# Local attention with its engine queues in another order: how six layers of a fused block on one NeuronCore respond

## The reference, cut to what matters

```python
qkv = x @ Wqkv                       # 128 -> 3 * 1024, 16 heads of 64
q = l2norm(q) * qs;  k = l2norm(k) * ksc
q = q * cos * scale + rotate_half(q) * sin * scale
k = k * cos / scale + rotate_half(k) * sin / scale
# windows of 32 tokens; each sees its own window and the one before
sim = einsum(q, k) * 8;  sim = where(mask, -big, sim)
out = einsum(softmax(sim), v)        # mask: it < jb or it > jb + 32
x = out @ Wo + x
```

## Time and profile before

| | |
|---|---|
| time of three runs | 8583.95, 8584.15, 8587.62 us; median 8584.15 |
| profiled execution | 8596.22 us, of which the span is 8594.4 us |
| period of one of the six layers | 530 to 531 us |
| one unit of attention in the steady part | 12.77 us |
| granted TensorE clock, whole span | 0.774 of full speed |

### The profile page before, as it was taken

The page is one execution under the profiler, slowest core; times in us unless marked ns, Lnnn a source line. Parts: engine busy times, 40 slices in busy tenths (PEclk is TensorE's granted clock), DMA queues, the critical chain, the costliest instruction groups (busy, mean ns, idle before and its releaser), DMA issues. The chain is left out here.

```text
span 8594.4 us, 84244 instructions
## 1 busy us (share of the span) xinstructions
PE 6067.9 (71%) x22816; PEld 3551.2 (41%) x22816; DVE 5534.0 (64%) x10124; ACT 3038.5 (35%) x6978; POOL 2830.0 (33%) x2050
## 2 busy tenths in 40 slices
PE   3686877868678686677766775677777775887554
PEld 1453544535455354122212221244555443665332
DVE  6775766757577575599848996477878776121334
ACT  1563655636456364100020001133333322333333
POOL 0452534525355252244413441044444442000000
PEclk6897989979899898699969997755555555555777
DMA  0000000000000000000000000000000000000000
GB/s 11 17 1 14 1 1 14 1 14 1 2 13 1 14 1 6 1 0 0 0 5 0 0 0 0 14 1 0 0 0 0 0 1 4 0 0 8 3 3 8
DMA packets 3953, 34.57 MB, mean 4 GB/s; under 512 B 401, under 2 KB 785, under 8 KB 2065
## 3 DMA queue, kind: packets, MB, share of 16 engines
q1 hardware_dynamic: 3600, 30.63, 1.0%
HBM read 29.58 MB, written 1.05 MB: 4 GB/s over the span
## 5 line engine op out<-in xcount | busy, mean ns | idle before, releaser
L744 POOL TENSOR_TENSOR slabs<-slabs 128x512 f32<-128x512 f32 x768 | 1034.7, 1377 | 1546.2 <-DVE slabs L680 1546.2
L1078 DVE TENSOR_TENSOR_SCAN slabs<-slabs 128x512 f32<-128x512 f32 x512 | 884.9, 1728 | 124.6 <-POOL slabs L1094 111.1
L1359 DVE MAX8 slabs<-slabs 128x8 f32<-128x512 f32 x1152 | 740.5, 687 | 295.1 <-ACT slabs L1310 285.3
L1094 POOL TENSOR_TENSOR slabs<-slabs 128x512 f32<-128x512 f32 x512 | 648.2, 1266 | 742.9 <-PE psum L1035 476.6
L1035 PE MATMUL psum<-slabs 128*128 128x512 f32 x1024 | 578.1, 646 | 296.5 <-POOL slabs L1094 296.5
L1393 POOL TENSOR_SCALAR slabs<-slabs 128x512 f32<-128x512 f32 x256 | 399.6, 1561 | 1043.0 <-DVE slabs L1366 1043.0
L629 ACT ACTIVATE slabs<-slabs 128x96 f32<-128x96 f32 x1536 | 553.0, 361 | 387.6 <-DVE slabs L709 387.6
L1275 PEld LDWEIGHTS psum<-slabs 128*128 128x128 f32 x3072 | 677.4, 333 | 7.5 <-ACT slabs L1301 7.5
L1275 PE MATMUL psum<-slabs 128*128 128x9 f32 (+1 forms) x3072 | 663.0, 359 | 0.0
L1261 PE MATMUL psum<-slabs 8*128 8x512 f32 (+1 forms) x768 | 596.9, 1136 | 79.7 <-DVE slabs L1342 58.5
L1269 PE MATMUL psum<-constants,slabs 128*128 128x128 f32 x1536 | 419.1, 433 | 274.3 <-POOL slabs L1397 263.7
(11 more groups left out here) (332 smaller groups left out, 11270.6 us busy)
## 6 DMA issues: line engine op xcount, KB each, us to landing
slabs<-F SPq DMA_DIRECT2D x6, 2756.5 KB, 10.2
weights<-S SPq DMA_DIRECT2D x4, 645.0 KB, 3.8
weights<-M SPq DMA_DIRECT2D x1, 2184.0 KB, 9.1
weights<-R SPq DMA_DIRECT2D x2, 1079.5 KB, 5.0
slabs<-x SPq DMA_DIRECT2D x1, 1024.0 KB, 4.8
slabs<-falloff SPq DMA_DIRECT2D x1, 1024.0 KB, 4.7
out<-slabs SPq DMA_DIRECT2D x1, 1024.0 KB, 3.9
weights<-L SPq DMA_DIRECT2D x1, 840.0 KB, 4.5
```

Of the source, the lines that this page charges most:

```text
L744: nc.gpsimd.tensor_tensor(out[:, at, :], normed[:, at, :], table, ALU.mult).then_inc(rope_done, 1)
L1078: nc.vector.tensor_tensor_scan(state[b % 2][:, 1:SEQ + 1], decay[:, cols(b)], fed[b % 2], 0.0, ALU.mult, ALU.add).then_inc(state_ready, 1)
L1094: nc.gpsimd.tensor_tensor(read[b % 2], r[:, cols(b)], state[b % 2][:, 0:SEQ], ALU.mult).then_inc(read_ready, 1)
L1359: nc.vector.max(eight, wk if k else s).then_inc(top_step, 1)
```

## The change

Four queues are reordered; no instruction is added or removed.

- PE: in iteration i `weigh` moves from the end of the iteration to the place between `turn_roped` and `score`, and works on unit i-3 instead of i-2. `values` moves from that place to the end.
- ACT: `square` comes first. `copy_values` works on unit i-1 and stands between `square` and `copy_turned`. `copy_context` moves from the head to behind `copy_turned`.
- DVE: `rope` for the keys of unit i and `total` for unit i-1 both stand at the end of iteration i. Written out, the sequence differs from that before in one thing: the reciprocal follows the key addition and no longer precedes it.

POOL's queue is the same.

```diff
# PE
-                if i < UNITS:
-                    values(i)
+                if i >= 3:
+                    weigh(i - 3)
                 if 1 <= i <= UNITS:
                     score(i - 1)
                 if 2 <= i <= UNITS + 1:
                     turn_probs(i - 2)
                 if i >= 3 and (i - 3) % 2 == 1:
                     project_out(i - 3)
-                if 2 <= i <= UNITS + 1:
-                    weigh(i - 2)
+                if i < UNITS:
+                    values(i)
# ACT
-                if i >= 3:
-                    copy_context(i - 3)
                 if i < UNITS:
                     square(i)
                 if 1 <= i <= UNITS:
+                    copy_values(i - 1)
                     copy_turned(i - 1)
-                if i < UNITS:
-                    copy_values(i)
+                if i >= 3:
+                    copy_context(i - 3)
                 if 2 <= i <= UNITS + 1:
                     copy_probs(i - 2)
# DVE
-                if 2 <= i <= UNITS + 1:
-                    total(i - 2)
-                if 1 <= i <= UNITS:
-                    rope(i - 1, 1, k_roped)
                 if i < UNITS:
                     normalise(i)
...
                 if i < UNITS:
                     rope(i, 0, q_roped)
+                    rope(i, 1, k_roped)
+                if 1 <= i <= UNITS:
+                    total(i - 1)
```

## The result

| | before | changed |
|---|---|---|
| median | 8587.62 us (5 runs, 8583.95 to 8590.67) | 8527.42 us (5 runs, 8515.90 to 8544.51) |
| ratio | | 0.9933, 95% interval 0.9918 to 0.9948 |
| profiled span | 8594.4 us | 8537.9 us |
| granted clock, whole span | 0.774 | 0.757 |

The change gains 60 us, 0.7%. The forecast was 154 us, and the measured time lies 27 us above the upper end of the range (8500).

The account below looks back on a forecast made before the run. A DVE and ACT loop of 12.78 us a unit was taken as the bound; per layer -26.1, -1.7 and +1.3 make -26.5, six layers -159, port +5: -154 us, forecast 8430 us, range 8395 to 8500.

Parts of the forecast that it names:

- The clock falls: Rival: new short pauses before weigh and key transposes halve PE's clock, +3.4 us a unit, kernel slower; chance 0.07.
- the 0.07: Chance given to the rival in which PE's clock falls and the kernel becomes slower.
- The clock was 1.00 through the steady part with pauses too: Argument against the falling-clock rival: PE in the kernel before had pauses, yet held full clock.
- PE's busy share rises: Argument against the falling-clock rival: PE's busy share goes from 0.81 to 0.88.
- Square first: ACT: square ahead of copy_context takes 1.21 us out of the loop, 12.78 to 11.57 us.
- Scores against the mask: PE to DVE: scores ready at 5.87 us after square's start, mask at 5.97; 0.1 us slack, lateness taken as 0.
- Project late in even iterations: PE: project, behind project_out and values, ends 0.5 us late in even iterations; pair 12.1 + 11.57 = 23.67 us.
- Copies moved back on ACT: ACT: copy_context done at 5.2 us and copy_probs at 7.75, both before the exponentials at about 8.7; no cost.
- The reciprocal behind the key addition: DVE and POOL: later finish_probs may delay small steps 0 to 0.35 us; 0.06 taken per odd unit, 5 us in all.
- keys gain some 0.1 us that nobody waits for: DVE: key addition ahead of the reciprocal gives turn_roped's keys some 0.1 us, with no effect on time.
- First and last units: Ends of each layer's attention: start -1.7 us (bounds 0 and -3.4), end +1.3 us (bounds -1.7 and +1.8).

Follow-up runs that it names:

- the fill: Changed kernel plus five unread products per unit on PE, two before the key-addition wait and three before weigh: 8394.62 us, ratio 0.9782.
- the five kernels of the table: Changed kernel without its DVE part 8573.5 us; as is 8527.4; with unread products before keys 8427.8, before weigh 8412.0, at both places 8394.6.

## Why the prediction was wrong, step by step

**The step that failed** is "The clock falls", as it was weighed and not as it was described. Its place was right (new short pauses, before weigh and before the key transposes), its price was close (3.4 us a unit forecast; 15.10 - 11.99 = 3.1 measured for a full dip, 13.62 - 11.99 = 1.6 for a partial one), and its threshold too: I put break-even at 8 of 28 units at half clock, and with 53 dips in six layers, 9 of 28, some of them partial, three quarters of the gain went. What was wrong is the 0.07, and both arguments for it. "The clock was 1.00 through the steady part with pauses too" compared single pauses: before there was one of 1.40 us ahead of the key transposes as well, but values stood right behind it. The trace of before shows it (L498 project, L509 the key transposes, L520 values; the scores follow at 385.10):

```profile
378.21 1.88 PE L498 MATMUL psum<-slabs 128*128 128x512 f32 x4
380.09 0.66 PE L506 MATMUL psum<-constants,slabs 128*128 128x128 f32 x4
382.15 0.66 PE L509 MATMUL psum<-constants,slabs 128*128 128x128 f32 x4 [1.40 <-DVE slabs L688]
382.65 1.88 PE L520 MATMUL psum<-slabs 128*96 128x512 f32 x4
```

The change put weigh there, which waits itself, and so three pauses came to stand with only eight transposes between them. "PE's busy share rises" compared averages over a unit, and rising it did (294.61 of 340 us, 0.87, some of it matmuls at half clock), while of the 3.45 us ahead of weigh 2.14 were idle. The rival was also bound to "and the kernel is slower": no case stood for a clock that falls in a third of the units and takes part of the gain, which is what came.

The Trainium skill, page "TensorE: Matmul & The Clock Gate", section "A second HAM failure mode: psum-queue depth-cycling", which the prediction set aside, says that short idles between groups of matmuls make the clock oscillate. The trace of the changed kernel agrees, with 0.50 and 1.00 in turn; the trace of before, with its pauses spread, held 1.00.

In numbers per layer: without dips the 28 intervals would take 14 x (11.54 + 11.99) = 329.4 us, 28.1 less than before, where I forecast 26.1. Measured they take 28 x 12.50 = 350.0. The dips cost 20.6 us a layer, 123 us in all. The spans of the profiled executions without and with the fill, 8537.9 and 8391.8 us, lie 146 us apart: 123 us are these intervals, and some 22 are the first three intervals of each layer, where the fill holds the clock too (in the first layer 1.00 between 270 and 300 us, against 0.79 in the changed kernel and 0.87 before).

**Square first:** right. The odd interval was forecast at 11.57 and is 11.54.

**Scores against the mask:** the tie held. With the first fill, in the steady part of the first layer, the mask never waits for the scores except once, at the layer's end.

**Project late in even iterations:** right, 0.45 us for the 0.5 forecast; the run with values behind project and the fill shows it, all intervals at 11.54.

**Copies moved back on ACT:** right as far as the time goes: the intervals of 11.54 us leave no room for a wait on them.

**The reciprocal behind the key addition:** right in the loop (1.47 us for finish_probs, L669's successor in the new file still 0.17 us, no effect alone), wrong in "keys gain some 0.1 us that nobody waits for". PE waited for them, 1.20 us with this part and 1.41 without, and with it the clock fell less often: 46 us.

**First and last units:** forecast -1.7 and +1.3 us a layer, measured about -0.4 for the first three intervals (38.0 for 38.4 us) and -0.6 for the rest. The layer period fell from 530.7 to 522.2 us: -7.5 - 0.4 - 0.6. The start was held back by the clock: with the fill its three intervals take 34.3 us.

## What to carry to other kernels

When a reordering takes slack out of a loop, list TensorE's waits in the new order one after the other, not only their sum or the busy share: where several of them come to stand with little work between, the clock may fall, and the matmuls in the loop take nearly twice as long (3.75 us for 2.02 here). The cheap test is to put harmless products into those waits; if the kernel gets faster with more work and the rows show the granted clock up, the clock was the loss. And try the parts of a reordering alone: here one part gave 150 us, all of them 60.

## What the runs showed of the hardware

A shift of 0.2 us between two of PE's waits, with their sum the same (2.14 us), went with 66 dips in place of 53 of 84 even intervals and with a time 46 us longer. The longest pause does not order the five kernels of the table (1.20 us stands beside 53 dips and beside none), and the sum of the waits leaves the first two equal; how length, sum and place act together was not settled. Nor is it settled why each dip of 15 us is followed by one of 13.6 in the next even interval, or why the first of them stands at different places in different layers. Transposes as filler held the clock as well as products did. POOL's scaling took 1.82 us where a VectorE addition with two SBUF inputs overlapped it and 1.47 us where none did.
